# Attention and 4-bit FFN on one core: the causal mask of the row maxima by VectorE in PSUM, table parts on ScalarE and GpSimd, another narrow output place

## What is computed

```python
xn = layernorm(x)
q, k, v = xn @ wq, xn @ wk, xn @ wv            # 32 heads of 32, 8 key/value heads; q and k are rotated (rope)
attn = softmax(q @ k.T / sqrt(32) + causal_mask)
s = (attn @ v) @ wo
w_gu = sc[g_idx] * (wq4 - (zq4[g_idx] + 1))    # 4-bit weights, 8 groups of rows, 1024 x 5504
h = silu(xn @ w_gate) * (xn @ w_up)            # 2752 wide
g = silu(h @ w_d)                              # w_d is 4-bit too, 21 groups
out = x + s * g
```

## Time and profile before

| what | value |
|---|---|
| median of 3 runs | 2408.37 us (2407.87 to 2408.56) |
| the profiled execution: its own time | 2408.08 us |
| its span, first to last instruction | 2405.9 us |
| granted TensorE clock, mean of the span | 0.986 of full speed |
| PE busy | 2309.3 us, 96% |
| PEld busy | 1183.5 us, 49% |
| DVE busy | 1214.0 us, 50% |
| ACT busy | 919.7 us, 38% |
| POOL busy | 1170.0 us, 49% |

### The profile page before, as it was taken

The page is one execution under the profiler, slowest core; times in us unless marked ns, Lnnn a source line. Parts: engine busy times, 40 slices in busy tenths (PEclk is TensorE's granted clock), DMA queues, the critical chain, the costliest instruction groups (busy, mean ns, idle before and its releaser), DMA issues. The chain is left out here.

```text
span 2405.9 us, 40989 instructions
## 1 busy us (share of the span) xinstructions
PE 2309.3 (96%) x16296; PEld 1183.5 (49%) x16296; DVE 1214.0 (50%) x1812; ACT 919.7 (38%) x1745; POOL 1170.0 (49%) x1280
## 2 busy tenths in 40 slices
PE   7999969999999999999999999999789999999999
PEld 4455425555555555555555555444344444444443
DVE  6688466766676766677766663453312121212100
ACT  3322126656656656556566655232211010101000
POOL 3555337777777777777777776332201010101000
PEclk9999969999999999999999999999999999999999
DMA  6242302122222122222212222333373131313120
GB/s 183 87 94 74 88 12 49 54 63 73 57 67 71 56 58 76 53 68 72 62 52 76 53 55 60 88 104 82 80 266 118 59 117 59 117 59 117 41 82 18
DMA packets 229103, 187.60 MB, mean 78 GB/s; under 512 B 121617, under 2 KB 200954, under 8 KB 228544
## 3 DMA queue, kind: packets, MB, share of 16 engines
q1 hardware_dynamic: 228928, 185.22, 26.7%
HBM read 113.18 MB, written 71.86 MB: 77 GB/s over the span
## 5 line engine op out<-in xcount | busy, mean ns | idle before, releaser
L1062 PE MATMUL gu_ps<-xT,wg 128*128 128x512 f16 x4128 | 985.4, 379 | 1.7 <-ACT h L1135 1.7
L1375 POOL TENSOR_TENSOR room<-room 128x1152 f16<-128x1152 f32 x256 | 539.6, 2108 | 60.6 <-ACT room L1094 57.4
L1062 PEld LDWEIGHTS gu_ps<-xT,wg 128*128 128x128 f16 x4128 | 367.7, 97 | 382.9 <-ACT h L1135 3.0
L1094 ACT ACTIVATE room<-sc_ps 128x512 f32<-128x512 f32 (+3 forms) x768 | 349.2, 489 | 438.3 <-PE sc_ps L987 437.5
L1777 POOL TENSOR_TENSOR room<-room 128x512 f32<-128x512 f32 x32 | 52.7, 1652 | 617.6 <-DVE room L1738 617.6
L1592 PE MATMUL dn_ps<-xT,hT_in 128*128 128x512 f16 x1536 | 337.3, 380 | 0.0
L1207 DVE TENSOR_REDUCE shift<-mx_ps 128x2 f16<-128x1024 f32 (+2 forms) x252 | 209.4, 831 | 152.7 <-PE mx_ps L969 148.1
L1738 DVE TENSOR_TENSOR room<-room 128x512 f32<-128x512 f32 x32 | 24.0, 754 | 428.7 <-ACT room L1666 428.6
L1592 PEld LDWEIGHTS dn_ps<-xT,hT_in 128*128 128x128 f16 x1536 | 148.8, 98 | 181.6 <-issue 7.5
L1370 POOL TENSOR_SCALAR_AFFINE_SELECT room<-room 128x128 f32<-128x128 f32 x512 | 144.3, 293 | 166.1 <-ACT room L1094 166.1
L654 PE MATMUL qk_ps<-xT,w 128*128 128x512 f16 x960 | 211.8, 381 | 6.0 <-ACT xT L424 4.6
(11 more groups left out here) (129 smaller groups left out, 2948.7 us busy)
## 6 DMA issues: line engine op xcount, KB each, us to landing
hidden_scratch<-hT SPq DMA_DIRECT2D x84, 256.0 KB, 3.0
hT_in<-hidden_scratch SPq DMA_DIRECT2D x16, 1344.0 KB, 5.8
o_scratch<-room SPq DMA_DIRECT2D x16, 1040.0 KB, 6.1
room<-o_scratch SPq DMA_DIRECT2D x16, 1040.0 KB, 8.1
arena<-q_scratch SPq DMA_DIRECT2D x48, 256.0 KB, 3.7
stock<-in_qw_d SPq DMA_DIRECT2D x42, 256.0 KB
down_scratch<-wd SPq DMA_DIRECT2D x84, 128.0 KB, 2.8
xin<-in_x SPq DMA_DIRECT2D x16, 512.0 KB, 4.3
```

The costliest lines, as they stand in the source:

```text
L1062: last = pe.matmul(to[:, :], wg[:, u, wp, s, cols], xT[:, xp, s, tokens], start=(s == 0 and k == 0), stop=(s == KT - 1 and k == 2))
L1094: act.activation(probs[:, r % 2, START[t] + c:START[t] + e], sc_ps[n % SC_BANKS][:, 0:e - c], ACT.Exp, scale=float(1.0 / np.sqrt(HD))).the ...
L1375: pool.tensor_tensor(p_lo[:, r % 2, c], probs[:, r % 2, c], p_hi[:, r % 2, c], ALU.subtract).then_inc(lo_done, 1)
```

## The change

1. **Mask.** The two mask matmuls of a diagonal piece (line 969) go: 16 for each pair of heads, 512 in all. Ahead of the reduction DVE adds the mask, 128 partitions by 2x128 float32, in place in PSUM, with the bfloat16 mask from SBUF, and waits for its own semaphore `masked`: 8 for each pair, 256 in all.
2. **Order of the pieces.** MAXIMA changes so that slots 0 and 4 always get a diagonal piece and the 1024-wide `part` pieces follow in slots 1 and 5.
3. **Outputs.** The narrow place goes to query tile 0, which only key tile 0 reaches.
4. **Tables of the middle stage.** DVE's three operations go. POOL subtracts all of `rest - mid` at the end of t = 2, ACT copies the low rows at t = 3, slot 1, and makes the zero points at t = 3, slot 3 by two copies from bytes. For that, stage one splits the packed zero points once into low and high nibbles (four DVE operations) and stores them to a DRAM scratch; the loads of each tile bring two halves (five DMAs instead of four).
5. **Tables of stage one.** Two byte copies in place of eight shifts and a copy, for four tables.

```diff
-TABLE = 7
+TABLE = 6
 def load_scales(...):
-    sp.dma_start(zw[0:G_GU, u, :, 0:w // NIB], zeros_gu...).then_inc(gu_loaded[u], 16)
+    for h in range(2):
+        first = h * (INTER // NIB) + j * (P // NIB)
+        sp.dma_start(zw[0:G_GU, u, :, h, 0:w // NIB], z_d[:, :, first:first + w // NIB]).then_inc(gu_loaded[u], 16)
 def build_table(...):
     if part == 3:
         dve.wait_ge(step, first + 5)
-        for k in range(NIB):
-            last = dve.tensor_scalar(whole[:, :, :, k], words, 4 * k, 15, ALU.logical_shift_right, ALU.bitwise_and)
+        for o in range(2):
+            last = dve.tensor_copy(zeros.rearrange("g h (c o) -> g h c o", o=2)[:, :, :, o], words[:, o].bitcast(U8))
         last.then_inc(step, 1)
-        dve.wait_ge(step, first + 6)
-        dve.tensor_copy(zeros, whole.rearrange("g h c k -> g h (c k)")).then_inc(step, 1)
 # project_qkv, SP
                 if e == CT + 2:
+                    sp.wait_ge(zeros_split, 2)
+                    sp.dma_start(z_d, gu_zs).then_inc(z_stored, 16)
+                if e == CT + 3:
                     sp.wait_ge(stock_zeroed, 1)
+                    sp.wait_ge(z_stored, 16)
 # project_qkv, DVE, at e == CT
+            def split_zeros():
+                dve.wait_ge(zw_loaded, 32)
+                for words, to in ((gu_zw, gu_zs), (tb_zw, tb_zs.rearrange("p o n h c -> p o (n h c)"))):
+                    for o in range(2):
+                        last = dve.tensor_scalar(to[:, o], words, 4 * o, 0x0F0F0F0F,
+                                                 ALU.logical_shift_right, ALU.bitwise_and)
+                    last.then_inc(zeros_split, 1)
 # attend_and_expand
-    MAXIMA = [(7, 0), (7, 1), (0, 0), (6, 0), (6, 1), (1, 0), (5, 0), (2, 0), (5, 1), (4, 0), (3, 0), (4, 1)]
+    MAXIMA = [(7, 1), (7, 0), (0, 0), (6, 1), (6, 0), (1, 0), (2, 0), (5, 0), (5, 1), (3, 0), (4, 0), (4, 1)]
-    WIDE = BANK // VW
+    WIDE = ST - 1
 # PE, maxima
-                diagonal = end == (t + 1) * P
                 for e in range(2):
                     last = pe.matmul(to[:, e, 0:end - first], qT[0:STACK, u, q + e, t * P:(t + 1) * P],
-                                     kT[0:STACK, u, first:end], start=True, stop=not diagonal)
-                if diagonal:
-                    for e in range(2):
-                        last = pe.matmul(to[:, e, t * P - first:end - first], identb[:, :], maskb[:, :],
-                                         start=False, stop=True)
+                                     kT[0:STACK, u, first:end], start=True, stop=True)
 # PE, outputs
-                    c = min(t, WIDE) * VW + max(t - WIDE, 0) * VH
+                    c = (t - 1) % ST * VW
-                    if t < WIDE:
+                    if t > 0:
 # ACT
+                act.activation(mid[:, :, 0:w], rest[:, :, 0:w], ACT.Copy)
                 act.activation(szt[32:64, u, 0, :, 0:w], rest[32:64, :, 0:w], ACT.Copy).then_inc(table_step, 1)
+            def table_low(j, u):
+                w, first = tile_width(j), TABLE * (D_TABLES + j)
+                act.wait_ge(table_step, first + 4)
+                act.activation(szt[64:R_GU, u, 0, :, 0:w], mid[64:R_GU, :, 0:w], ACT.Copy).then_inc(table_step, 1)
+            def table_zeros(j, u):
+                w = tile_width(j)
+                for o in range(2):
+                    to = szt[0:G_GU, u, 1, :, 0:w].rearrange("g h (c o) -> g h c o", o=2)
+                    last = act.activation(to[:, :, :, o], zw[0:G_GU, u, o, :, 0:w // NIB].bitcast(U8), ACT.Copy)
+                last.then_inc(table_step, 1)
 # DVE, maxima
+                banks = maxima_banks(m, r, k)
+                if width + c * BANK == (t + 1) * P:
+                    to, block = shift[:, p, :, t], banks[:, :, width - P:width]
+                    dve.tensor_tensor(block, block, maskb[:, :].unsqueeze(1).to_broadcast([P, 2, P]), ALU.add
+                                      ).then_inc(masked, 1)
+                    dve.wait_ge(masked, ST * n + sum(c0 == t0 * P // BANK for t0, c0 in MAXIMA[:k + 1]))
+                else:
+                    to = part[:, p, :, t - BANK // P]
+                dve.tensor_reduce(to, banks[:, :, 0:width], AX_X, ALU.max, negate=True).then_inc(mx_taken, 1)
 # POOL
+            def table_low(j):
+                w, first = tile_width(j), TABLE * (D_TABLES + j)
+                pool.wait_ge(table_step, first + 3)
+                pool.tensor_tensor(mid[:, :, 0:w], rest[:, :, 0:w], mid[:, :, 0:w], ALU.subtract).then_inc(table_step, 1)
```

More of the change, by code:

```diff
@@ L137, in load_groups, with build_table @@
                  ).then_inc(idx_loaded, 16)
-def build_table(dve, step, first, part, raw, hold, rest, mid, words, whole, zeros):
+def build_table(dve, step, first, part, raw, hold, rest, mid, words, zeros):
     rows = raw.shape[0]
@@ L575, in tables_at @@
                     if k % 4 == 0:
-                        dve.wait_ge(gu_loaded[u], 64)
-                    gate_up_table(dve, table_step, TABLE * (NP + u), k % 4, scw, zw, szt, rest, mid, zn, u, u)
+                        dve.wait_ge(gu_loaded[u], 80)
+                    gate_up_table(dve, table_step, TABLE * (NP + u), k % 4, scw, zw, szt, rest, mid, u, u)
                 if 8 <= k < 12:
@@ L746, in attend_and_expand @@
         mx_ready = sem("mx_ready")
+        masked = sem("masked")
         mx_taken = sem("mx_taken")
@@ L1168, in tables @@
                     if (t, at_slot) == (2, 1):
-                        table_parts(j + 2, u)
+                        table_mid(j + 2, u)
+                    if (t, at_slot) == (3, 1):
+                        table_low(j + 2, u)
+                    if (t, at_slot) == (3, 3):
+                        table_zeros(j + 2, u)
             def wo_high(m, r):
@@ L1205, in maxima @@
                     dve.wait_ge(shift_turned, n)
-                to = shift[:, p, :, t] if width + c * BANK == (t + 1) * P else part[:, p, :, t - BANK // P]
-                dve.tensor_reduce(to, maxima_banks(m, r, k)[:, :, 0:width], AX_X, ALU.max, negate=True).then_inc(mx_taken, 1)
+                banks = maxima_banks(m, r, k)
[7 more added lines that the diff above has]
+                dve.tensor_reduce(to, banks[:, :, 0:width], AX_X, ALU.max, negate=True).then_inc(mx_taken, 1)
                 if k == NM - 1:
@@ L1348, in step @@
                     select(m, r, i)
-                    tables(m, r, i)
                 wo_low(m, r)
@@ L1354, in _ @@
             for q in range(REP):
-                last = dve.memset(o[:, :, WIDE, q * VW + VH:(q + 1) * VW], 0.0)
+                last = dve.memset(o[:, :, 0, q * VW + VH:(q + 1) * VW], 0.0)
             last.then_inc(zeros_set, 1)
@@ L1408, in table_rest, with tables @@
                                    ).then_inc(table_step, 1)
+            def table_low(j):
+                w, first = tile_width(j), TABLE * (D_TABLES + j)
+                pool.wait_ge(table_step, first + 3)
+                pool.tensor_tensor(mid[:, :, 0:w], rest[:, :, 0:w], mid[:, :, 0:w], ALU.subtract).then_inc(table_step, 1)
+            def tables(m, r):
+                if not unit(m, r):
+                    return
+                j, u, t = unit(m, r)
+                if j + 2 < FTILES and t == 1:
+                    table_rest(j + 2, u)
+                if j + 2 < FTILES and t == 2:
+                    table_low(j + 2)
             def step(m, r):
@@ L1419, in step @@
                 lows(m, r, 5)
-                table_rest(m, r)
+                tables(m, r)
             steps(step)
@@ L1845, in build @@
                     arena, lanes_in, sc_gu, qz_gu, sc_dn, qz_d, gi_gu, lanes, szd, sel_gu, w_in, qw_gu, qw_d, gi_d,
-                    qwg, zw, scw, szt, rest, mid, zn, qwd, idx, gu_loaded, dn_loaded, idx_loaded, table_step,
-                    qw_loaded)
+                    qwg, zw, scw, szt, rest, mid, qwd, idx, gu_loaded, dn_loaded, idx_loaded, table_step,
+                    qw_loaded, z_d)
         COLS = sum(S - t * P for t in range(ST))
```

114 lines of the change are left out of this document (38 added, 76 removed).

## The result

The changed kernel takes 2365.19 us (median of 4 runs, 2362.39 to 2365.58) against 2408.47 beside it on the same chip: 0.9818 of the time before, 95% interval [0.9801, 0.9835]. That is 1.8% faster. The forecast was 2355.5, so 9.7 us too low: inside its range of 2347 to 2378, but above the 2350 to 2361 that the forecast itself had. The profiled execution took 2362.39 us, where the sum gave 2355.2.

The account below looks back on a forecast made before the run. PE was taken to set the pace. From the profiled 2408.08 us: -27.0 masks, -9.0 outputs, -23.1 tables, +3.2 adds, +3.5 lead-in, -0.5 stage one gave 2355.2, or 2355.5 as median; forecast 2350 to 2361, range 2347 to 2378.

Parts of the forecast that it names:

- The four-step length: Middle stage, four steps of one FFN tile with heads: about 68.4 us claimed in place of 71.82.
- The rival in which POOL holds the add: DVE's mask add, reading SBUF, is held by POOL and takes 1.4 us more; about 2528 us, chance 0.04.
- Masks, adds, outputs: Middle-stage terms: mask matmuls off PE -27.0 us, DVE adds in the steps +3.2, 448 fewer output matmuls -9.0.
- The lead-in: Stretch ahead of the first scores, where DVE is the limit: eight adds of the first pair, taken at +3.5 us.
- The 98 ns rival: PE's mask matmuls each cost their 98 ns weight load, not 55 ns; 2334 us, halfway 2345, chance 0.06.
- that of POOL or ACT as the pace: Middle-stage steps: POOL or ACT set the pace and half the gain goes; 2380 to 2400 us, chance 0.04.
- the first one: Rival on DVE's adds: handover slower than 0.45 us, 2368.6 at 0.65, 2378 at 0.75; 2361 to 2380, chance 0.24.
- SP waits for one small store: Stage one, SP's DMA queue: the added wait was named within a stage-one term of 0 to -1.5 us.
- Stage one ... I take -0.5: Stage one: shorter tables give back at most PE's 1.5 us wait for DVE; 0 to -1.5, taken as -0.5 us.
- the band that the prediction gave to slower adds: Rival on DVE's mask adds in the steps: slower handover to the reduction, 2361 to 2380 us, chance 0.24.
- All three operations go, so the 1.54 us of each tile go: DVE's table work in the middle stage: PE's three losses per tile vanish, 15 x 1.54 = -23.1 us.
- The third rival: DVE's mask add waits for POOL: 162 us more in four chained slots, 11 in the lead-in; chance 0.04.

Follow-up runs that it names:

- e5: The changed kernel with the mask matmuls back on PE and no adds on DVE; 2384.83 us, 0.9895 of the time before.
- e4: The changed kernel with the narrow output place back at query tile 7, 448 more narrow matmuls; 2372.24 us, 0.9846.
- e6: The changed kernel with SP's store of the split zero points and its burst of table loads each issued one round earlier; 2357.06 us, 0.9782.
- e1: The kernel before with only the mask moved to DVE adds; old piece order, outputs, tables and stage one; 2375.66 us, 0.9859.
- e2: The kernel before with mask adds on DVE, new piece order and new output place, table work as before; 2398.96 us, 0.9956.
- e10: The kernel before with mask adds on DVE and the new output place, but old piece order, tables and stage one; 2369.24 us, 0.9834.

## Why the prediction was right, and where it was off

**Right: direction, range and mechanism.** PE set the pace, and what went from PE came off the time. The four-step length was worked out at 68.2 (about 68.4 with a little for ACT, which did not come) and is 68.18; PE waits at slot 1 of odd steps by 0.11 us (0.10) and at no table place. The add was taken at 0.45 from its start to the reduction's, and it is 0.46; the mean is 429 ns. The rival in which POOL holds the add falls with that mean over 252 of them. The Trainium skill (SBUF — State Buffer, SBUF: two separate sides) names only operations with two SBUF inputs, or in a two-port mode, as the ones that contend; the traces agree in both halves: the add with one operand in PSUM stays at 429 ns, `table_picks` with two in SBUF goes from 405 to 1831.

**Masks, adds, outputs: right.** 23.8 forecast and 22.3 measured by taking them away (e5), 9.0 and 8.5 (e4). The lead-in was +2.4 for +3.5. Of the steps' -55.9, 1.7 us are missing, about what these two terms fell short. The 98 ns rival and that of POOL or ACT as the pace fall too, by e5 and by PE's waits. Two rivals are slightly misadded: at 0.75 us the first one's terms give 2379 and not 2378, and the third counts again the 0.10 us at odd slot 0 that the sum holds already, 3 of its 173 us.

**Off: "SP waits for one small store" and "Stage one ... I take -0.5".** This is the mis-sized term: +6.2 instead of -0.5, nearly all of the 7.2 us between the sum and the profiled execution. The step named the wait and did not say what is queued behind it. What lay behind were 14 table loads, some 10 us of SP's queue, and behind those the load of x and the store of v, for which ACT and then PE wait. e6 takes 5.95 us of it away with the same work; 1.7 us more are of a clock that the profiled execution of before had been granted near 102 us; some 1.5 us that the rest of the new stage one gives back stand against them. The remaining 2.5 us between 9.7 and 7.2 are the profiled execution's own distance from its median. Four of the six profiles with this stage one end it 1.2 to 1.7 us later than it, at the lower clock behind PE's wait; whether the executions without a profile did so is not shown.

**Luck in the range.** The measured 2365.2 lies outside the 2350 to 2361 of the forecast. It lies in the band that the prediction gave to slower adds, with a chance of 0.24, and the adds were not slower. So the range held because it was widened for a cost that did not come, and one that it had at nothing, SP's queue, took its place.

**Right in sum, wrong in kind: "All three operations go, so the 1.54 us of each tile go".** They do go, and the total of the steps holds. But 1.54 us is not the price of having tables on DVE. That is 9.8 us with the old order and 40.9 with the new one, with masks and outputs changed in both. The third rival knew that POOL holds these operations, but the sum took the losses as fixed. They hang on whether DVE or POOL starts first, and e1 (8 us below its expectation) shows that an edit elsewhere changes it. By the prediction's steps e2 and e10, with masks, adds and outputs but the tables left, would both take 2408 - 27 - 9 + 3.2 + 3.5 = 2379 us. They took 2399 and 2369.

**Open.** Why the clock near 102 us is 2.4 GHz throughout in two profiles and not in eleven was not tried. In those two PE had been idle for 2.7 us ahead of it, in the others for 2.8 to 4.4. What gives back the 1.5 us in stage one (the byte copies, or the other placing of the loads) was not told apart.

## What to carry to other kernels

When a wait is put into the list of an engine that issues DMAs, read on in that list: price the burst behind it issue by issue, and look for the first store in it that frees a buffer. An operation's duration that is four times that of its neighbours of equal size is not its own; ask who holds it, and expect it to jump when any edit shifts the phase. And test terms from both ends, by taking each away from the changed kernel and by adding it to the old one: the terms that agree are prices, the others are properties of a schedule.

## What the runs showed of the hardware

- An 8x256 operation of DVE with both operands in SBUF took 0.41 us when it started 0.05 us ahead of POOL's 128x1152 subtraction, and 2.21 when it started 0.17 behind it; POOL's then took 2.33 and 2.11. In before, e1, e2 and e10, 15 tiles each, its length goes by this order every time.
- The combination of `shift` and `part`, 128x8 with both in SBUF, went from 164 ns on average before to 762 after. It had not been in the forecast, and PE waits for none of it. Group and timeline of after:

```profile
L1248 DVE TENSOR_TENSOR shift<-shift,part 128x8 f16<-128x8 f16 x32 | 24.4, 762 | 1.1
```

```profile
439.62 1.17 DVE L1248 TENSOR_TENSOR shift<-shift,part 128x8 f16<-128x8 f16 x1
```

- An addition in place in PSUM, 128x256 float32 with a bfloat16 operand from SBUF, takes 429 ns, and 293 for half the size. Two halves in a row take 0.48 to 0.50 us together.
- A wait of PE of 5.34 to 5.36 us was followed by a stretch (170 to 190 us) with a clock of 0.91 or 0.83 in six profiles of six, one of 0.93 to 1.90 us by 1.00 in seven of seven.
